# A transformer block on one Trainium2 core: attention with row-tiled scores and probabilities transposed by DMA

## The reference

```
x = x + attn(layernorm(x)) ;  x = x + ffn(layernorm(x))
attn: q, k, v = x @ Wqkv (16 heads of 32) ; a = softmax(causal(q k^T / sqrt(32))) ; (a v) @ Wo
ffn:  h1 = x @ q(w1)^T ; h3 = x @ q(w3)^T ; (silu(h1) * h3) @ q(w2)^T     (1365 hidden features)
q(w): s = mean(|w|) ; clip(round(w / s), -1, 1) * s
```

## Time and profile before

| | us |
|---|---|
| median of three runs (lowest, highest) | 572.34 (571.48, 573.64) |
| span of the profiled execution | 570.0 |
| PE busy | 540.9 (95%) |
| DVE busy | 373.7 (66%) |
| POOL busy | 289.8 (51%) |
| ACT busy | 265.0 (46%) |

### The profile page before, as it was taken

How to read it: one execution, slowest core, us unless ns; L and a number is a source line. 1 busy time by engine, 2 the same in 40 slices (tenths; PEclk the granted TensorE clock), 3 DMA queues, 4 the chain that set the end, 5 groups by cost and what they waited for, 6 DMA issues and landing times.

```text
span 570.0 us, 8957 instructions
## 1 busy us (share of the span) xinstructions
PE 540.9 (95%) x3180; PEld 252.7 (44%) x3180; DVE 373.7 (66%) x937; ACT 265.0 (46%) x437; POOL 289.8 (51%) x339
## 2 busy tenths in 40 slices
PE   3899789999999999999999999999989999999997
PEld 3444334344444445444444444444434444444443
DVE  7797798988986766615786757565774645554421
ACT  4877688848263636232353635431235743013320
POOL 5152799687544558400747284701448787113320
PEclk9999799999999999999999999999999999999999
DMA  8979969677852030035573012214230001150001
GB/s 330 321 166 264 215 173 249 181 164 153 176 140 73 1 93 21 1 93 148 131 127 97 18 36 59 75 37 132 74 57 1 3 0 56 38 129 1 0 20 55
DMA packets 82880, 58.52 MB, mean 103 GB/s; under 512 B 51434, under 2 KB 71914, under 8 KB 82836
## 3 DMA queue, kind: packets, MB, share of 16 engines
q1 hardware_dynamic: 82836, 57.95, 38.8%
HBM read 33.55 MB, written 12.58 MB: 81 GB/s over the span
## 4 chain that ended last, share of the span: by engine, by line
PE 63%; POOL 11%; DVE 10%; DMA 6%; ACT 4%; SPq 3%; issue 3%; DVEq 0%; ACTq 0%
PE work L1092 38%; PE work L1272 13%; PE score_bank L1167 4%; PE prob_bank L1189 3%; POOL early L650 3%; PE work L1210 3%; POOL early L641 2%; POOL early L653 2%; DMA early<-in_L_ffn_w 2%; ACT early L755 2%; PE work L1232 2%; DVE masked L954 2%; DVE rows L929 1%; POOL early L675 1%; DMA late<-rows 1%
## 5 line engine op out<-in xcount | busy, mean ns | idle before, releaser
L1092 PE MATMUL work<-late,w_ternary 128*128 128x512 f16 (+1 forms) x704 | 160.4, 379 | 1.3 <-DMA late<-rows 0.8
L755 ACT ACTIVATE early<-prob_bank,scalars 128x512 f32<-128x512 f32 x160 | 100.3, 683 | 98.6 <-PE prob_bank L1189 98.4
L954 DVE CUSTOM_DVE_ANT_0 masked<-score_bank,mask 128x512 f16<-128x512 f32 (+3 forms) x256 | 111.6, 485 | 26.6 <-PE score_bank L1167 26.2
L1092 PEld LDWEIGHTS work<-late,w_ternary 128*128 128x128 f16 (+1 forms) x704 | 68.9, 100 | 77.6 <-issue 2.2
L667 POOL TENSOR_TENSOR late<-late 128x512 f16<-128x512 f32 (+1 forms) x44 | 50.6, 1157 | 60.2 <-ACT late L775 60.2
L641 POOL TENSOR_SCALAR_AFFINE_SELECT early<-early 128x640 f32<-128x640 f32 (+2 forms) x96 | 43.7, 486 | 72.9 <-ACT early L755 72.9
L1272 PE MATMUL work<-w_ternary,late 128*128 128x512 f16 (+1 forms) x352 | 78.0, 379 | 0.0
L990 DVE SCALAR_TENSOR_TENSOR late<-late,work 128x512 f32<-128x512 f32 (+1 forms) x44 | 30.2, 686 | 52.3 <-ACT late L768 52.2
L1092 PE MATMUL work<-xt,wqkv_hi 128*128 128x512 f16 x192 | 57.2, 380 | 2.6 <-DVE wqkv_lo L909 1.4
L650 POOL TENSOR_TENSOR early<-early 128x768 f32<-128x768 f32 x32 | 58.4, 1826 | 2.0
L1167 PE MATMUL score_bank<-k_stack,q_stack 96*128 96x512 f16 (+3 forms) x256 | 51.0, 305 | 4.9 <-DMA k_stack<-k_lo_spill 2.5
(11 more groups left out here) (112 smaller groups left out, 761.0 us busy)
## 6 DMA issues: line engine op xcount, KB each, us to landing
rows<-in_L_attn_x SPq DMA_DIRECT2D x16, 256.0 KB, 3.0
q_stack<-q_hi_spill SPq DMA_DIRECT2D x32, 128.0 KB, 2.6
k_stack<-k_hi_spill SPq DMA_DIRECT2D x32, 128.0 KB, 3.0
x_res<-in_L_attn_x SPq DMA_DIRECT2D x12, 256.0 KB, 3.0
out_y<-x_res SPq DMA_DIRECT2D x12, 256.0 KB, 2.2
late<-in_L_ffn_w SPq DMA_DIRECT2D x4, 682.5 KB, 4.4
early<-in_L_ffn_w SPq DMA_DIRECT2D x3, 768.0 KB, 12.2
late<-in_L_ffn_w SPq DMA_DIRECT2D x3, 768.0 KB, 4.9
```

What stands on the lines that cost most here:

```text
L755: act.activation(probs[:, u, :], prob_bank[u % 2][:], ACT.Exp, scale=scalar(exp_scale)).then_inc(prob_free, 1)
L954: dve.tensor_tensor_reduce(masked[:, k % 2, 0:n], score_bank[u % 2][:, off:off + n], mask[:, S - n:S], 1.0, LOWEST, ALU.add, ALU.max, row_ ...
L1092: last = pe.matmul(bank, lhs, rhs, start=(n == 0), stop=(n == len(terms) - 1))
```

## The change

It rewrites the attention and all five lists. The names of steps that stay keep their work, except as said here.

- Scores: q and k are no longer spilled and stacked. The halves stay in three buffers each (`HALVES`), and each head's 32 rows are used where they lie, so a head's matmul uses 32 rows of the PE array. Each head has its own PSUM bank. A slot has three fills: 512, 384 + 128, and 256 columns for each head.
- Maxima: DVE also scales the scores and writes them as float32 into one of four SBUF buffers (`RAWS`). POOL makes the exponential's bias from the maxima (`bias`), ACT takes the exponential in place with the row sum as a side result (`exp`), ACT (first fill) or DVE (the others) makes the float16 high half (`high`), POOL the low half (`low`).
- SP turns the halves of the four heads by one DMA per fill (`probs_turn`: 32, 32 and 16 blocks of 128x128 float16, 80 per slot).
- Values: three float16 products (v is split as well) in place of the float32 ones. The row sums are inverted as a 128x16 tile, spread by PE (`inverse`), copied by ACT and multiplied by DVE.
- The low half of the rows for `xt` and `yt` moves from DVE to POOL.
- PE's list near the end now reads `inverse:15 down:2,3 values:15 project:3,0-3 gate:3,0-1`, and `values:4` still comes ahead of `gate:0,0`, but only six slots' `scores` have begun by then (eight before) and q, k of slots 0 to 7 are made.

```diff
 def exp(s, p, h):                                   # ACT
+    act.wait_ge(bias_made, n // 2 + 1)
+    for j, (tile, off, cols) in enumerate(FILLS[p]):
+        piece = raws[n % RAWS][:, off:off + cols]
+        last = act.activation(piece, piece, ACT.Exp, bias=bias, accum_out=sums[:, s % 2, at:at + 1])
 def high(s, p, h):                                  # ACT for p = 0, DVE for p = 1, 2
+    if fill == 1: act.wait_ge(turned["w1"], 16 * len(TURNS["w1"]))
+    if fill > 1:  fill_turned(act, fill - 2)
+    act.activation(split_view(s, p, 0, h), raw_view(s, p, h), ACT.Copy)
 def low(s, p, h):                                   # POOL
+    pool.tensor_tensor(split_view(s, p, 1, h), raw_view(s, p, h), split_view(s, p, 0, h), ALU.subtract)
 def bias(s, p, h):                                  # POOL
+    pool.tensor_scalar(exp_bias[..., both], row_max[..., both], -1.0, LOG_UNIT, ALU.mult, ALU.add)
 def probs_turn(s, p):                               # SP
+    if s: full(sp, ("values", s - 1))
+    sp.wait_ge(low_done, HG * (fill + 1))
+    sp.dma_start_transpose(probs[:, TURNED_AT[p]:TURNED_AT[p] + BLOCKS[p], :], split_probs[fill % 2][...])
 def maxima(s, p, h):                                # DVE
+    if n >= RAWS: dve.wait_ge(low_done, n - RAWS + 1)
+    dve.tensor_tensor_reduce(raws[n % RAWS][:, off:off + cols], score_bank[h][:, off:off + cols],
+                             mask[:, S - cols:S], scalar(exp_scale), LOWEST, ALU.add, ALU.max, row_max[...])
 def scores(s, p):                                   # PE
-    last = pe.matmul(score_bank[u % 2][:, off:off + n], q[0:3 * HD, h, ...], k[0:3 * HD, h, 0:n], start=True, stop=True)
+    for j, (tile, off, cols) in enumerate(FILLS[p]):
+        for t, (a, b) in enumerate((("hi", "hi"), ("hi", "lo"), ("lo", "hi"))):
+            for h in range(HG):
+                heads = slice(HD * h, HD * (h + 1))
+                pe.matmul(score_bank[h][:, off:off + cols], half["q", a][s % HALVES][heads, ...],
+                          half["k", b][s % HALVES][heads, 0:cols], start=(t == 0), stop=(t == 2))
 def inverse_rows(step):                             # PE
+    for u in range(ST):
+        for h in range(HG):
+            pe.matmul(work[bank][HD * h:HD * (h + 1), u * P:(u + 1) * P], of_head, ident[:], ...)
 def values(step):                                   # PE
+    terms = [(kt, w, part_) for kt in range(ST) for w, part_ in ((v_hi, 0), (v_hi, 1), (v_lo, 0))]
```

More of the change, by code:

```diff
@@ L115 @@
[L115 to L118, removed]
+        stats_x:0,0-3 weight_round:w1,0-8 bias:0,0,1 weight_round:w1,9 bias:0,0,3 low:0,0,0 weight_round:w1,10
@@ L133 @@
[L133 to L137, removed]
@@ L186 @@
+        lin:3,5 gate:3,6 lin:3,6 gate:3,7 lin:3,7 gate:3,8 lin:3,8 gate:3,9 lin:3,9 gate:3,10 lin:3,10 down:3,2
+        down:3,0-1 down:3,3
     """,
     "pe": """
[L188 to L191 removed]
@@ L212 @@
-        gate:1,9 q:15 probs:11,4 lin:1,9 gate:1,10 scores:13,1 lin:1,10 values:11 scores:13,2 sums:11 probs:12,0
-        scores:13,3 down:1,0 probs:12,1 scores:13,4 down:1,1 max_row:13 probs:12,2 scores:14,0 down:1,2
-        probs:12,3 project:2,0 scores:14,1 v:3,0 probs:12,4 scores:14,2 project:2,1 scores:14,3 down:1,3
-        scores:14,4 project:2,2 max_row:14 scores:15,0 project:2,3 v:3,1-3 scores:15,1 values:12 scores:15,2
-        sums:12 probs:13,0 gate:2,0 probs:13,1 lin:2,0 probs:13,2 gate:2,1 probs:13,3 lin:2,1 probs:13,4
@@ L217 @@
-        gate:2,2 lin:2,2 gate:2,3 values:13 scores:15,3 sums:13 probs:14,0 lin:2,3 probs:14,1 gate:2,4
-        scores:15,4 probs:14,2 lin:2,4 probs:14,3 gate:2,5 probs:14,4 max_row:15 lin:2,5 gate:2,6 lin:2,6
-        values:14 sums:14 probs:15,0 gate:2,7 probs:15,1 lin:2,7 probs:15,2 gate:2,8 lin:2,8 probs:15,3 gate:2,9
-        probs:15,4 lin:2,9 gate:2,10 values:15 lin:2,10 sums:15 down:2,0-1 project:3,0-3 down:2,2-3 gate:3,0
-        lin:3,0 gate:3,1 lin:3,1 gate:3,2 lin:3,2 gate:3,3 lin:3,3 gate:3,4 lin:3,4 gate:3,5 lin:3,5 gate:3,6
@@ L223 @@
+        lin:3,8-9 gate:3,10 lin:3,10 down:3,0-3
     """,
@@ L243, in numbered @@
     return {step: n for n, step in enumerate(s for s in ORDER[engine] if s[0] in kinds)}
-WORK = numbered("pe", "top_turn", "weight_mean", "xt", "q", "k", "v", "max_row", "project", "gate", "lin", "down", "sums", "values")
-HALF = numbered("act", "xt", "yt", "q", "k", "max_row")
+WORK = numbered("pe", "top_turn", "weight_mean", "xt", "q", "k", "v", "project", "gate", "lin", "down", "inverse", "values")
+HALF = numbered("act", "xt", "yt", "q", "k", "v")
+HIGHS = {engine: numbered(engine, "high") for engine in ("act", "dve")}
 SPLIT = numbered("act", "split", "wo_split")
@@ L976, in project, with normalise @@
+            def normalise(s):
+                bank = bank_of(("values", s))
+                emptied(dve, ("inverse", s))
+                full(dve, ("values", s))
+                dve.tensor_tensor(o_sb[:], work[bank][:], o_sb[:], ALU.mult).then_inc(work_free[bank], 1)
             def project(step):
```

718 lines of the change are left out of this document (358 added, 360 removed).

## The result

The changed kernel takes 579.27 us (median of 4 runs, 577.91 to 580.09) against 572.65 of the kernel before in the same measurement: 1.0107 times, 95% interval 1.0085 to 1.0129. The forecast was 577.5. The profiled execution's span is 578.3 us, 8.3 above the 570.0 of before.

The account below looks back on a forecast made before the run. It took a chain over all engines to bound the stage up to 167.5 us, then PE's own work. 570.0 - 11.6 + 13.8 + 3.0 = 575.2 of span, plus 2.3: 577.5 us, range 552 to 606.

Parts of the forecast that it names:

- the likeliest case: The prediction's own forecast of 577.5 us, given a chance of 0.39 and a range of 567 to 588.
- T: Start of the first gate matmul, end of the early stage; 167.4 us before, forecast 170.4, +3.0.
- PE behind T: PE's work after the first gate matmul: scores, values, transposes, array changes and q, k together -11.6 us.
- The step from the span to the runs' median: Whole program: the runs' median lies 2.3 us above the profiled span, 575.2 to 577.5.
- 0.29 + 0.08: The two parts of the chance that the changed kernel is faster, rounded to 0.36.
- the DMA sum: DMA work ahead of T, with 80 turned blocks a slot: 165 to 190 us; lower sum at 0.96 gives 172.
- Rival 2: Early stage: DMA bounds it at its upper sum, T = 186 and time 593 us; chance 0.18.
- Rival 1: Slot 0 to project:0: earlier first exponentials shorten the early stage, T 157 and time 564 us; chance 0.30.
- The end, +13.8: Uncovered waits ahead of gate:3 (+9.4) and project:3 (+2.9), plus a lower clock (+1.5); range 8 to 18 us.
- 3 (loads of 32-row tiles): Scores on PE: weight loads don't overlap, 4.75 us a slot, +28, time 605 us; chance 0.09.
- 4 (row tiles in series): Scores on PE: row tiles don't run side by side, 6.4 us a slot, +45, time 622 us; chance 0.04.
- What would show it: Profile signs: PE near 500 busy, 75 idle; 9 to 11 us pause ahead of gate:3,0; 32-block turns in 6 to 8.

Follow-up runs that it names:

- edit 1: Changed kernel with half of each fill's blocks left out of the DMA transposes from slot 1 on: 579.56 us, 1.0117 times before.
- edit 12: Kernel of edit 7 with the second fill's high halves also on ScalarE in slots 1 to 5: 577.77 us, 1.0081 times before.
- Edit 6: Kernel before with down:2,2-3 moved from between project:3 and gate:3 to ahead of project:3: 585.19 us, 1.0204 times before.
- edit 7: Changed kernel with thrown-away PE products in the two pauses ahead of project:3 and gate:3: 577.67 us, 1.009 times before.
- edit 5: Changed kernel with down:2,2 moved between values:15 and project:3, and down:2,3 between project:3 and gate:3: 579.05 us, 1.012 times before.
- Edit 4: Changed kernel with the score matmuls of all four heads on the first 32 rows of the PE array: 652.37 us, 1.1377 times before.
- (8): Changed kernel with the first fill's high halves back on VectorE in all slots but slot 10: 613.03 us, 1.0675 times before.
- edits 3: Changed kernel with heads in the outer loop, so one head's three score products follow each other: 578.98 us.

## Why the prediction was right, step by step

- **Time.** 577.5 forecast, 579.27 measured; the likeliest case's own range was 567 to 588, "slower" the likeliest of the three outcomes. The mechanism at the end was right, but that the total is this near is luck. T came 8.8 us higher than forecast and PE behind T 8.8 lower, which cancels; the end came 3.1 higher. The step from the span to the runs' median, 2.3 in the forecast, was 1.0, since the profiled execution was the longest of the four runs. So the time came out 1.8 above the forecast. (In the chances, 0.29 + 0.08 is 0.37 and not 0.36; nothing hangs on it.)
- **T, +3.0: wrong, +11.8.** The step that failed is the one that set T by the DMA sum and by ACT's sum at DVE's share of 86%. The sums of ACT and POOL were well sized (140.6 for 145, 124.6 for 131); DMA's lies below its range (0.90 x 179.2 = 161 for 165 to 190), and DVE's was too small (130.1 for 115, since a copy takes 0.65 or 0.48 and a maximum with float32 output 0.74 where it took 0.69). But neither DMA's (1) nor ACT's (12) bounds the stage. No compute engine reaches 79%. Rival 2's T of 186 was nearer, with a mechanism that edit 1 refutes. The first slot is only 3.6 us late (its `values` start at 73.65, 70.09 before). Those of slots 1, 2 and 3 start at 96.33, 121.49 and 145.14, where they started at 86.22, 102.88 and 118.51: 26.6 us late by slot 3. Between there and T 14.8 come back, where the lists hold the scores of two slots fewer. The loss lies in the ring's waits and in the lower clock. The prediction named such chains as a danger for the stage behind T only, and took no clock into T. Rival 1's early exponentials are there (the first at 36.09, 55.55 before), but did not carry over.
- **PE behind T, -11.6: direction right, -20.4.** Scores take 1.6 us a slot and not 2.0, which is 4 us of it: I had leaned away from the hidden end for loads that hide fully. Two more are pauses that the earlier trace rows has and the changed kernel has not. The change between array modes is 0.09 where I took 0.1 (from 164.26 + 0.216 to 164.57). The remaining 3 us are spread over q, k, values and changes and were not told apart.
- **The end, +13.8: right in its parts, +16.95.** 9.98 us ahead of `gate:3` (9.4; its own terms, 8.8 and 0.5, make 9.3), 2.8 ahead of `project:3` (2.9), and 1.6 + 2.55 for the clock where I had 1.5, which no row had sized. Edit 6 shows the first with its clock in the kernel before, edit 7 the clock alone. What I did not see is that `down:2` is where it is because slot 15 is late (5).
- **Rivals.** 3 (loads of 32-row tiles) and 4 (row tiles in series) fall by the profile: twelve loads and twelve matmuls in 0.66 us. Edit 4 makes rival 4's case and shows its price: 73 us where I had said 45 behind T; it is 55.4 behind T and 15.9 ahead of it.
- **What would show it.** PE busy 506 (500) and idle 72 (75), 54 of them ahead of T; PE at 97% from T to 509.5; fills of 0.66 us; a turn lands 6.7 us after its issue in the median, 4.3 to 10.9. All as said, but for single turns ahead of T that took longer than the 6 to 8 us.
- **High halves on ScalarE in the first fill.** I had them only as sums of ACT and DVE. Their worth is in the place in DVE's list: without them the changed kernel is at 613 (8).

No version that does the whole computation beats the kernel before; the best are the two with filled pauses, edit 7 at 1.009 and edit 12 at 1.0081 times its time, which are level.

## What to carry to other kernels

Where no compute engine is over 80% busy and a full DMA queue proves not to bind, don't set the stage's length by the largest sum: follow one buffer through its steps, and ask for each step what stands behind it in its engine's list. An engine is chosen for a step by where the step must stand in the list, more than by whether the engine has room: the same 60 copies, nearly as long on either engine (0.62 and 0.65 us), were worth 34 us. Work between a producer and its last consumer at the end of a program hides a latency and keeps the clock; before moving it, see which other wait it covers.

## What the runs showed of the hardware

- Four row tiles of 32 rows run wholly side by side (0.22 us for four matmuls of 512 columns, 0.86 on the same rows), in either order of heads and terms. The loads of 128 columns by 32 rows overlap as well: twelve stand in the 0.66 us of a fill, which at 0.10 each in series would be 1.2. The Trainium skill (TensorE: Matmul & The Clock Gate, "LDWEIGHTS") has the load's time go by columns; the single load agrees, 0.10, but that section has nothing on loads side by side.
- Granted clock: after a pause of 9 to 10 us the next 176 matmuls took 40.5 to 41.0 us in seven kernels (37.99 in the earlier trace rows) and 39.5 in edits 3 and 8; after 5.33 us in edit 5 they took 40.98; with PE kept busy until 2.4 us or less ahead of them, 38.15. After a pause of 2.8 us, 48 matmuls took 10.5 to 12.2 (10.36).
- A turned block of 128x128 float16 costs about 0.19 us of all DMA engines: between 80 and 170 us edit 1 moved 12.64 MB where the changed kernel moved 17.34, which is 143 blocks of 32 KB fewer, and took (0.99 - 0.69) x 90 = 27 us of their time. The forecast had 0.175 to 0.215. The Trainium skill (DMA: Bandwidth & Descriptors, "Latency and other measured facts") would have 0.125 by its 261 GB/s, an estimate; the measurement decides, and here it moved the time by nothing.
